# Random-feature attention: one stream of 40 output units, output products inside the next tile, key features in place, squares in four column groups

## The reference

```python
def softmax_kernel(data, proj, is_query, eps=0.0001):
    data_dash = jnp.einsum('bhnd,md->bhnm', data * normalizer, proj)
    diag = jnp.sum(data ** 2, axis=-1, keepdims=True) * 0.5 * normalizer ** 2
    if is_query:
        m = jnp.max(data_dash, axis=-1, keepdims=True)
    else:
        m = jnp.max(data_dash, axis=(-2, -1), keepdims=True)
    return ratio * (jnp.exp(data_dash - diag - m) + eps)
...
    qp = softmax_kernel(q, proj[i], True)
    kp = softmax_kernel(k, proj[i], False)
    d_inv = 1.0 / jnp.einsum('bhnm,bhm->bhn', qp, k_sum)
    ctx = jnp.einsum('bhnm,bhnd->bhmd', kp, v)
    o = jnp.einsum('bhmd,bhnm,bhn->bhnd', ctx, qp, d_inv)
    x = x + o @ Wo[i] + bo[i]
```

## Time and profile before

| | us |
|---|---|
| median of 3 runs | 3040.56 |
| lowest, highest | 3040.13, 3047.05 |
| profiled execution | 3042.31 |
| its span | 3040.5 |

### The profile page before, as it was taken

The page is one execution under the profiler, slowest core; times in us unless marked ns, Lnnn a source line. Parts: engine busy times, 40 slices in busy tenths (PEclk is TensorE's granted clock), DMA queues, the critical chain, the costliest instruction groups (busy, mean ns, idle before and its releaser), DMA issues.

```text
span 3040.5 us, 27921 instructions
## 1 busy us (share of the span) xinstructions
PE 2645.5 (87%) x8756; PEld 1455.5 (48%) x8756; DVE 1529.6 (50%) x3729; ACT 701.9 (23%) x1525; POOL 1021.6 (34%) x833
## 2 busy tenths in 40 slices
PE   3998887999199999999898887898998999998877
PEld 2664555666044444444565545554454444443322
DVE  4556457999400000000225543357666676676664
ACT  1223222211021001100235222133233333322222
POOL 0006686666000000000000000055656665665665
PEclk9998998999699999999999998999999999999999
DMA  8911416777902230243000400088988988998898
GB/s 284 276 41 4 111 1 169 207 206 216 213 29 56 66 83 0 64 116 93 7 0 0 155 0 7 7 280 314 327 308 308 337 317 302 339 328 320 320 346 331
DMA packets 243106, 523.84 MB, mean 172 GB/s; under 512 B 98857, under 2 KB 99232, under 8 KB 238850
## 3 DMA queue, kind: packets, MB, share of 16 engines
q0 software_dynamic: 161392, 348.53, 34.6%
q1 hardware_dynamic: 79072, 169.12, 17.8%
q10 hardware_dynamic: 2550, 5.12, 0.5%
HBM read 489.51 MB, written 45.34 MB: 176 GB/s over the span
## 4 chain that ended last, share of the span: by engine, by line
PE 66%; DVE 14%; issue 7%; DMA 6%; ACT 3%; POOL 1%; SPq 1%; another core or an unknown queue 1%; DVEq 0%; ACTq 0%; POOLq 0%
PE bank L1256 13%; PE bank L1029 10%; PE bank L1014 5%; DVE qv L863 4%; PE bank L1236 4%; PE bank L1246 4%; PE bank L781 3%; PE bank L561 2%; PE bank L1193 2%; PE bank L1019 2%; PE bank L573 2%; PE bank L568 2%; PE bank L592 2%; PE bank L808 2%; PE bank L1205 2%
## 5 line engine op out<-in xcount | busy, mean ns | idle before, releaser
L1156 POOL MEMSET wreg<- 64x2048 f32 x2 | 3.6, 1802 | 1106.9 <-DVE h L711 1106.9
L1256 PE MATMUL bank<-qv,stage 125*125 125x512 f32 x640 | 340.2, 623 | 37.9 <-issue 15.7
L1337 ACT ACTIVATE stage<-ident,qv 125x125 f32<-125x125 f32 x640 | 246.4, 399 | 507.9 <-DVE qv L1490 175.1
L1490 DVE SCALAR_TENSOR_TENSOR qv<-qv 125x512 f32<-125x512 f32 x320 | 237.9, 750 | 152.6 <-DMA qv<-in_L_ffn_rows,qv 69.1
L863 DVE SCALAR_TENSOR_TENSOR qv<-wreg,att_b,qv 128x2048 f32<-128x2048 f32 x120 | 276.8, 2348 | 48.8 <-DMA wreg<-in_L_gnn_basis 42.3
L287 POOL DMA_INDIRECT adj<-e_cnt,e_idx x80 | 176.3, 2204 | 310.0 <-issue 273.6
L1162 POOL DMA_INDIRECT qv<-in_L_ffn_rows,qv x160 | 162.3, 1015 | 221.3 <-DVE qv L1432 113.0
L287 POOL DMA_INDIRECT adj_b<-e_cnt,e_idx x80 | 180.7, 2258 | 71.0 <-DMA adj<-e_cnt,e_idx 39.8
L1256 PEld LDWEIGHTS bank<-qv,stage 125*125 125x125 f32 x640 | 113.6, 193 | 184.0 <-issue 121.1
L1162 POOL DMA_INDIRECT qv<-in_L_ffn_rows,biasb x160 | 163.4, 1021 | 100.8 <-PE bank L1256 74.1
L1256 PE MATMUL bank<-big,stage 125*125 125x512 f32 x320 | 167.0, 617 | 13.3 <-issue 6.4
(11 more groups left out here) (222 smaller groups left out, 4167.6 us busy)
## 6 DMA issues: line engine op xcount, KB each, us to landing
wreg<-in_L_gnn_basis SPq DMA_DIRECT2D x60, 1024.0 KB
big<-in_L_mix_W SPq DMA_DIRECT2D x4, 4096.0 KB
adj<-adj_b POOLq DMA_DIRECT2D x9, 1328.1 KB, 40.9
adj<-wreg SPq DMA_DIRECT2D x5, 2187.5 KB
adj_b<-wreg SPq DMA_DIRECT2D x5, 2187.5 KB
wreg<-adj SPq DMA_DIRECT2D x10, 1093.8 KB
qv<-adj SPq DMA_DIRECT2D x10, 1093.8 KB
big<-cells_t SPq DMA_DIRECT2D x1, 10000.0 KB, 27.0
```

The source lines that it names most:

```text
L1256: nc.tensor.matmul(psum[7][0:P, :], diags[:, s % DRING, :], ring[s % RING][0:P, DIM:ROW], start=(s == 0), stop=(s == SLOTS - 1), skip_grou ...
L1337: nc.scalar.activation(diags[:, s % DRING, :], ident[0:P, 0:P], ACT.Relu, scale=inner[:, s:s + 1]).then_inc(p_diag, 1)
L1490: nc.vector.scalar_tensor_tensor(ring[s % RING][0:P, 0:DIM], ring[s % RING][0:P, 0:DIM], probs_of[t % 2].rearrange("p h k -> p (h k)")[:, ...
```

## The change

In attn1 the sums of squares are formed the other way round: `headsel` (32 columns) is the weight and the squares move, 250 columns, eight matmuls, head pair `c` into partitions `32c` to `32c+31` of bank 0. ScalarE copies that bank to `dgs`, four transposes bring it to bank 1, and VectorE's `spread` writes `diag`. `scale` runs after the fourth key copy, the normalization of the next pair is split around the second maximum, and the key product banks are taken in the order 4, 5, 6, 7. In attn2 the shift is the bias of eight exponentials per tile that work in place in `kdash`; the values are read where they lie; the two buffers, the copies, the subtractions and the zeroing matmuls go. The context's copies are split between VectorE and ScalarE, and its transposes stand inside attn3's second unit. attn3 is one stream of 40 units: transposes of tile T's output in unit 4T + 8, its product in 4T + 9, the residual in VectorE's unit 4T + 10. Bank 3 serves the output and every fourth unit's transposes, bank 2 the other three. The query columns are read in place. All these loops are unrolled.

```diff
-        headsel = sb("headsel", [128, KC, HEADS])
+        headsel = sb("headsel", [128, 32])
...
+        dgs = stage[:, 0:2 * PT]
         ctx_t = stage[0:HD + 1, 0:HEADS * FEATS]
-        v_st = view(ctx_flat, 0, [2, HEADS * (HD + 1)], P)
-        kfeat = view(stage, 0, [2, HEADS * FEATS], P)
-        q_st = view(stage, 0, [KC, PT])
...
-        KD_BANKS = (6, 7, 4, 5)
+        KD_BANKS = (4, 5, 6, 7)
...
+            def spread(i):
+                dve.wait_ge(m["dg_pe"], l * ADDS["dg_pe"] + i + 1)
...
+                    nc.vector.tensor_scalar(diag[:, 2 * i + j, :, :].rearrange("p s (c e) -> p s c e", c=KC),
+                                            psum[1][0:P, 256 * j:256 * j + 256].rearrange("p (s c w) -> p s c w", s=2, c=KC)[:, :, :, 0:2],
+                                            0.5 * NORM * NORM, None, ALU.mult).then_inc(m["dg"], 1)
...
+                    if n == 1:
+                        spread(i)
+                        if not last:
+                            norm1(2 * i + 2)
...
-            subtract_k(dve, l, 0)
-            subtract_k(dve, l, 1)
...
-                for j in range(2):
-                    for s in range(2):
-                        for c in range(KC):
-                            mm = nc.tensor.matmul(psum[0][0:P, 16 * j + 8 * s:16 * j + 8 * s + 8], sq[:, s, c, P * j:P * j + P],
-                                                  headsel[:, c, :], start=(c == 0), stop=(c == KC - 1), skip_group_check=True)
-                mm.then_inc(m["dg_pe"], 1)
-                pe.wait_ge(m["v"], l * ADDS["v"] + i * 2 + 2)
+                for s in range(2):
+                    for c in range(KC):
+                        mm = nc.tensor.matmul(psum[0][32 * c:32 * c + 32, PT * s:PT * s + PT], headsel[:, :], sq[:, s, c, :], start=True, stop=True,
+                                              skip_group_check=True)
+                mm.then_inc(m["dg_mm"], 1)
...
                     if n == 2:
-                        pe.wait_ge(m["k"], l * ADDS["k"] + i * KC + KC + 2)
-                    if n == 4 and not last:
+                        pe.wait_ge(m["dgc"], l * ADDS["dgc"] + i + 1)
+                        for jj in range(2):
+                            for s in range(2):
+                                mm = nc.tensor.transpose(psum[1][0:P, 256 * jj + 128 * s:256 * jj + 128 * s + 128],
+                                                         dgs[:, PT * s + P * jj:PT * s + P * jj + P], ident[:, :])
+                        mm.then_inc(m["dg_pe"], 1)
+                    if n == 4 and i < PAIRS - 1:
...
+                act.wait_ge(m["dg_mm"], l * ADDS["dg_mm"] + i + 1)
+                nc.scalar.activation(dgs, psum[0][:, 0:2 * PT], ACT.Copy).then_inc(m["dgc"], 1)
...
-                    if n == 5 and not last:
+                    if n == 3 and i < PAIRS - 1:
...
-                    nc.scalar.activation(v_st[:, j, :], v_aug[:, ds(i * 2 + j, 1), :, :].rearrange("p o h d -> p (o h d)"), ACT.Copy)
-                    act.wait_ge(m["ksub"], l * ADDS["ksub"] + i * 2 + j + 1)
-                    nc.scalar.activation(kfeat[:, j, :], sq1(kdash[:, ds(i * 2 + j, 1), :]), ACT.Exp).then_inc(m["kx"], 1)
...
+            for t in range(TILES):
+                for hh in range(HEADS):
+                    kt = kdash[:, t, FEATS * hh:FEATS * hh + FEATS]
+                    op = nc.scalar.activation(kt, kt, ACT.Exp, bias=kshift[:, t, hh:hh + 1])
+                    if hh % 4 == 3:
+                        op.then_inc(m["kx"], 1)
...
+            for t in range(TILES):
+                for b in range(2):
+                    dve.wait_ge(m["kx"], l * ADDS["kx"] + 2 * t + b + 1)
+                    kt = kdash[:, t, 1024 * b:1024 * b + 1024]
+                    nc.vector.tensor_scalar(kt, kt, EPS_K, None, ALU.add).then_inc(m["kf"], 1)
...
-            for b in range(4):
-                nc.tensor.matmul(psum[b][:, :], zeros[:, :], wreg[:, 0, 0:512], start=True, stop=False, skip_group_check=True)
...
+            return 3 if u % KC == 1 else 2
...
+            def normalize(T, b):
+                dve.wait_ge(m["o_pe"], l * ADDS["o_pe"] + 2 * T + b + 1)
+                got = psum[4 + b][0:P, 0:4 * (HD + 1)].rearrange("p (h d) -> p h d", h=4)
+                nc.vector.reciprocal(rden[:, T % 2, 4 * b:4 * b + 4].unsqueeze(2), got[:, :, HD:HD + 1]).then_inc(m["rd"], 1)
+                dve.wait_ge(m["rd"], l * ADDS["rd"] + 2 * T + b + 1)
+                nc.vector.tensor_tensor(o_sb[:, T % 2, 256 * b:256 * b + 256].rearrange("p (h d) -> p h d", h=4), got[:, :, 0:HD],
+                                        rden[:, T % 2, 4 * b:4 * b + 4].unsqueeze(2).to_broadcast([P, 4, HD]), ALU.mult).then_inc(m["o"], 1)
+
+            def residual(T):
+                dve.wait_ge(m["at_pe"], l * ADDS["at_pe"] + T + 1)
+                nc.vector.tensor_tensor(h[:, T, :], psum[3][0:P, :], h[:, T, :], ALU.add).then_inc(m["hat"], 1)
+                dve.wait_ge(m["hat"], l * ADDS["hat"] + 2 * T + 3)
+                nc.vector.tensor_tensor(h[:, T, :], h[:, T, :], b_o, ALU.add).then_inc(m["hat"], 1)
+
+            for n in range(UNITS + 7):
+                if n < UNITS:
+                    T, c = n // KC, n % KC
+                    dve.wait_ge(m["qd_pe"], l * ADDS["qd_pe"] + n + 1)
+                    nc.vector.tensor_reduce(qmax[:, n % 4, :], psum[QD_BANKS[n % 4]][0:P, :].rearrange("p (s m) -> p s m", s=2), AX, ALU.max).then_inc(m["qm"], 1)
+                    dve.wait_ge(m["qm"], l * ADDS["qm"] + n + 1)
+                    nc.vector.scalar_tensor_tensor(qneg[:, n % 4, :], qmax[:, n % 4, :], -1.0, diag[:, T, 0, 2 * c:2 * c + 2],
+                                                   ALU.mult, ALU.subtract).then_inc(m["qn"], 1)
+                if n == 1:
+                    for b in (0, 2):
+                        dve.wait_ge(m["cT_pe"], l * ADDS["cT_pe"] + b + 1)
+                        to, got = context_out(b)
+                        nc.vector.tensor_copy(to, got).then_inc(m["ctx"], 1)
+                if 2 <= n < UNITS + 2:
+                    u = n - 2
+                    dve.wait_ge(m["qT_pe"], l * ADDS["qT_pe"] + u + 5)
+                    nc.vector.tensor_scalar(qfeat_t[:, u % 2, :], psum[turn_bank(u)][:, 0:4 * P], EPS_K, None, ALU.add).then_inc(m["qT"], 1)
+                if n >= 4 and n % 2 == 0 and (n - 4) // 4 < TILES:
+                    normalize((n - 4) // 4, (n - 4) % 4 // 2)
+                if n >= 10 and n % 4 == 2:
+                    residual((n - 10) // 4)
...
+                if n >= 8 and n % 4 == 0:
+                    T = (n - 8) // 4
+                    act.wait_ge(m["oT_pe"], l * ADDS["oT_pe"] + T + 1)
+                    nc.scalar.activation(o_t[:, T % 2, :], psum[3][:, 0:4 * P], ACT.Copy).then_inc(m["oT"], 1)
...
-                out_proj(0)
-                out_mm(0)
-                out_proj(1)
-                out_mm(1)
...
+            def out_turn(T):
+                pe.wait_ge(m["o"], l * ADDS["o"] + 2 * T + 4)
+                if T < TILES - 1:
+                    pe.wait_ge(m["qT"], l * ADDS["qT"] + 4 * T + 8)
+                else:
+                    pe.wait_ge(m["hat"], l * ADDS["hat"] + 2 * T + 1)
+                for k in range(KC):
+                    mm = nc.tensor.transpose(psum[3][:, P * k:P * k + P], o_sb[:, T % 2, 128 * k:128 * k + 128], ident[0:P, 0:P])
+                mm.then_inc(m["oT_pe"], 1)
+
+            def out_mm(T):
+                pe.wait_ge(m["oT"], l * ADDS["oT"] + T + 2)
+                if T == 0:
+                    pe.wait_ge(m["w"], l * ADDS["w"] + W_LOADS + 16)
+                for k in range(KC):
+                    mm = nc.tensor.matmul(psum[3][0:P, :], o_t[:, T % 2, P * k:P * k + P], wreg[:, 3, 512 * k:512 * k + 512],
+                                          start=(k == 0), stop=(k == KC - 1))
+                mm.then_inc(m["at_pe"], 1)
...
+                    if u % KC == 1 and u >= 9:
+                        pe.wait_ge(m["hat"], l * ADDS["hat"] + 2 * ((u - 9) // 4) + 3)
+                    elif u:
+                        pe.wait_ge(m["qT"], l * ADDS["qT"] + u + (1 if u % KC in (1, 2) else 2))
...
+                if n >= 8 and n % 4 == 0:
+                    out_turn((n - 8) // 4)
+                if n >= 9 and n % 4 == 1:
+                    out_mm((n - 9) // 4)
```

More of the change, by code:

```diff
@@ L485, in pair @@
                     nc.vector.tensor_scalar(k_t[:, c, :], psum[4 + c % 2][:, 0:PT], c_bk[:, c:c + 1], None, ALU.add).then_inc(m["k"], 1)
-                    if l == 0 and not first:
+                    if l == 0 and i:
                         merge_dve(dve, i, c * CHUNK // KC, CHUNK // KC)
@@ L554, in turn @@
                     mm.then_inc(m["yT_pe"], 1)
-            def pair(i, last):
+            turn(0)
+            for i in range(PAIRS):
+                kd0 = l * ADDS["kd"] + 4 + 8 * (i - 1)
                 pe.wait_ge(m["yT"], l * ADDS["yT"] + i * KC + KC)
@@ L630, in attn1_act @@
[L630 to L632 removed]
```

(29 more changed lines are left out.)

270 lines of the change are left out of this document (92 added, 178 removed).

## The result

| | before | after |
|---|---|---|
| median | 3043.48 us (4 runs) | 2889.28 us (4 runs) |
| lowest, highest | 3040.13, 3047.05 | 2852.70, 2895.53 |
| profiled execution | 3042.31 | 2895.53 |
| its span | 3040.5 | 2893.7 |

The time fell by 154 us by the medians and by 146.8 us by the two profiled spans. The ratio is 0.945, with a 95% interval of 0.936 to 0.954, formed without the profiled run of 2895.53 us, which counts as slow because it lies 1.5% above the lowest; the next run, 2895.20 us, is in it. The forecast was 2881 us (2855 to 2926). One thing strikes at once: the runs of before lie within 7 us, those of after are spread over 43.

What follows compares the result with a forecast made beforehand. TensorE's chain was taken to bound both attention layers, with VectorE's bases and GpSimd's adjacency followed after layer 0. Gains of 58.0 (layer 1), 73.0 (layer 0) and 29.0 us sum to 160.0, giving 2881 us, range 2855 to 2926.

Steps and rivals of the forecast that it cites:

- Squares and the turn: First attention loop: squares 1.4 us, TensorE's 1.78 us idle goes, pair 29.9 us; gains 18.7 us (layer 1), 27.6 (layer 0).
- Rival (a): First attention loop: column groups do not overlap, ten pairs cost 2.0 us more each, 2901 us; chance 0.17.
- lower clock that I kept in reserve: First attention loop, layer 1: one dip of TensorE's clock kept in the estimate, 2 us.
- Features: attn2: key features in place, no buffer waits, first product waits 2.7 us, sum 40.8 us; gains 9.1 and 10.7 us.
- Outputs: attn3 as one stream: tile pitch 13.7 us with one 1.2 us stop on VectorE's residual; gains 34.7 and 30.2 us.
- (c): attn3: bound by the round trip through VectorE and ScalarE, one more unit a tile, 43 us: 2924 us; chance 0.12.
- (d): Better than forecast: no clock dips, no stall on bank 3, 10 + 19 us, 2852 us; chance 0.08.
- (e): attn3: output stream at the lower clock, 12.5 us more a tile, 3131 us, slower than before; chance 0.02.
- The bases: After layer 0's attention: GpSimd's sums start near 712, after the last base is issued, so VectorE's 42.3 us waits go.
- Rival (b): After layer 0: sums start near 682, the last three bases wait 10 us each as before, 2911 us; chance 0.15.
- The loads behind the sums: Next stage's root, bias and first tiles (1.75 MB) take 26 us beside the sums: 13.3 given back, net gain 29.0 us.

Runs made afterwards that it cites:

- before_hold: The kernel before the change, with GpSimd's ten adjacency sums held until the first graph network tiles have landed: 2982.3 us, ratio 0.990.
- gate_early: The changed kernel with layer 0's two gate weight loads issued before the bases instead of between root and bias: 2858.3 us, ratio 0.947.
- split_loads: gate_early with the bias load and the tile loads (125 partitions each) cut into 112 and 13 partitions: 2831.4 us, ratio 0.938.
- after_again: The changed kernel run once more, nothing edited, beside other kernels on one chip: 2867 us, 2824 to 2879.

## Why the prediction was right where it was, and wrong where it was not

**The total.** 2889 us against 2881. That it fits is in part luck, in errors that cancel: the attention gave 20.6 us more than forecast, the stage between the layers 50.6 us less, and stages for which nothing was forecast 16.8 us more.

**Squares and the turn.** Right in mechanism, and near in size: 0.98 + 0.19 us against the 1.4 that I took. The pair was forecast at 29.9 us and is 29.72; no q product waits, no turn waits. The Trainium skill's two rules ("TensorEngine Tiling (Array Packing)", Theoretical Speedup and Key Properties) both hold as far as the rows show: of a fourfold gain 3.4-fold is there, 3.38 to 0.98 us, and if the 0.19 us behind the squares are the drain, it takes back 0.19 of 2.40. Rival (a) is out. Of the lower clock that I kept in reserve nothing was seen in layer 1.

**Features.** Right. The products' wait was forecast at 2.7 us and is 3.0; the products took 37.3 us with 2.5 us of cold clock forecast in 38.1. With the first loop, layer 1 gained 32.6 us to its last context product (forecast 27.8) and layer 0 44.6 us (38.3). Of the 4.8 us more in layer 1, 2 are the dip that did not come; the rest is spread over the pairs, their end and the products.

**Outputs.** Right, with the stop at the forecast place: 0.64 us a tile instead of 1.2, pitch 13.30 instead of 13.7. From the end of an output product (1612.43) TensorE reached the wait after 3.2 us (forecast 3.0) and VectorE's addition ended after 3.7 (forecast 4.1). Layer 1 gained 34.0 us (30.2), layer 0 40.0 us (34.7). Rivals (c) and (d) are out, and (e) with them: a tile at the lower clock would have taken 25 us.

**The bases.** Right. The scatters began at 213 instead of 219 and took 3.3 us each beside the bases (forecast 3.4), so the sums started at 699 and not 712, still behind the last base. The waits of 42.3 us went; the bases took 314.8 us from 389.7 on (forecast 313). Rival (b) is out: during attention a scatter took 2.60 us (68 from 213 to 390), not 2.3. (Its ten scatters at 3.4 us would have put the sums at 678, not 682.) And before_hold shows that the waits were the sums'.

**The loads behind the sums.** This is the step that failed: "at that rate these take 26 us: 13.3 us given back". It was priced by bytes, at the rate of a base. It took 78.6 us from the last residual to the first product, against 16.4 before: 62 us given back. (A smaller error stands beside it: the 12.7 us that I took for the first product of before run only to TensorE's first transposes of the tiles.) The rate of a base was a true number for a base, which is 512 packets on 16 engines, 32 each, and at some 0.48 us for a packet of each queue that is the 15 us that I had read. Applied to bytes it misses that the two gate loads, 4 KB, are 64 packets an engine (19.5 us by gate_early), and that bias and tiles put 75 packets on each of five engines (56.4 us without the gates in gate_early, 32.9 with both loads cut in split_loads). The count by engine was there to be made from the loads' shapes; I looked at the sizes alone.

**Not forecast.** The memory stage was 14.5 us shorter, though nothing of it was changed. Profiled on the second chip it was 1152.3 us in before_hold and 1149.4 in after_again; in all nine later profiles of kernels made from the changed one, on three chips, it is 1144 to 1149. On the first chip it was 1179 and 1164. So the stage differs by 20 us and more between chips, and only 3 us of difference between the kernels are seen where both ran on one; the rest of the 14.5 I leave open.

## What to carry to other kernels

When a change moves a burst of large transfers onto a stretch where small loads are wanted, count those loads in packets for each engine they use, not in bytes: pieces per engine times the time of one packet of each queue. Here a load with 125 partitions used five engines; with bias and tiles cut into 112 and 13, root, bias and tiles together took 32.9 us beside the sums instead of 56.4. And where a gain comes from taking a wait away, follow what is issued next: here 42 us of waits on one engine went, and 62 us came back on another, for one line's worth of order between two queues. The spread of the runs had grown with the change, from 7 us to 43, and where it was 55 one line that fixed the order brought it to 3: such a new spread is worth following up as a possible sign of a race.

## What the runs showed of the hardware

- Beside each other, the two queues advanced by equal counts of packets (428 and 428, 347 and 350, 361 and 365), with 4 bytes or 2 KB in the one and some 4.7 KB in the other.
- A load of 125 partitions: 5 packets more than its pieces, and 31.4% of 16 engines busy while it ran alone, which is five engines.
- 500 KB of tiles took 9.8 us behind the other loads alone, and 27 us beside the sums. The Trainium skill says of turns that an engine drains a whole packet of several descriptors before it changes queues ("DMA: Bandwidth & Descriptors", Queues, rings and completion order); the equal counts here would also come of such turns of equal length, and the traces cannot tell the two apart.
- Four groups of 32 columns, fp32 with 250 moving columns each: 0.98 us for eight matmuls, 3.38 us without groups.
- With one operation of 0.67 us moved from in front of VectorE's residual addition to behind it, a tile took 12.68 us instead of 13.30.
